# One more mix of half 1 on TensorE, and a new order of the work at the start on every engine

## The reference

```python
# layer 0: eight 256x256 weights mixed by cond, masked
w = einsum('bg,got->bot', cond, weight * mask)
x = x + (einsum('bnt,bot->bno', x, w) + bias)
# layer 1: a shared gated MLP and the best 2 of 8 experts by cond, inner size 1024
rw = softmax(cond); w, sel = top_k(rw, 2); w = w / w.sum()
x = x + mlp(x, shared) + sum_k w_k * mlp(x, expert[sel_k])
# mlp(x) = (gelu_tanh(x @ gate) * (x @ up)) @ down
```

## Time and profile before

| | us |
|---|---|
| median of 3 runs (lowest, highest) | 412.96 (412.57, 413.46) |
| profiled execution, its own time | 412.5 |
| its span | 410.7 |
| PE busy | 405.5 |
| POOL busy | 313.2 |
| DVE busy | 306.8 |
| ACT busy | 252.8 |

### The profile page before, as it was taken

One profiled execution on the slowest core, in us unless ns is written; L12 is line 12 of the kernel. 1 busy time (PEld: TensorE's weight loads), 2 busy tenths in 40 slices (PEclk: granted clock), 3 DMA queues, 4 the chain that ended last, 5 costly groups with the idle time before them and its releaser, 6 DMA issues.

```text
span 410.7 us, 7438 instructions
## 1 busy us (share of the span) xinstructions
PE 405.5 (99%) x2236; PEld 352.7 (86%) x2236; DVE 306.8 (75%) x516; ACT 252.8 (62%) x482; POOL 313.2 (76%) x322
## 2 busy tenths in 40 slices
PE   8999999999999999999999999999999999999997
PEld 5788888888888988888889888888888888888886
DVE  5778886586658887767677879857687677677784
ACT  5687677565565668555655666757455656676541
POOL 1699999999719689999635879999670977999630
PEclk9999999999999999999999999999999999999999
DMA  8543342333200622333000152222201042241101
GB/s 297 205 138 97 120 104 91 102 86 98 75 4 7 190 60 86 122 105 102 28 26 1 51 184 97 77 77 98 81 26 27 0 130 76 77 129 54 51 1 53
DMA packets 18895, 35.23 MB, mean 86 GB/s; under 512 B 2098, under 2 KB 2610, under 8 KB 18866
## 3 DMA queue, kind: packets, MB, share of 16 engines
q1 hardware_dynamic: 18576, 34.61, 26.7%
q10 hardware_dynamic: 290, 0.26, 0.2%
HBM read 32.77 MB, written 2.10 MB: 85 GB/s over the span
## 4 chain that ended last, share of the span: by engine, by line
PE 97%; DVE 2%; issue 0%; ACT 0%; POOL 0%; DVEq 0%; POOLq 0%
PE o_ps L582 16%; PE p_ps L582 12%; PE g_ps L528 11%; PE u_ps L527 11%; PE u_ps L531 10%; PE u_ps L528 10%; PE g_ps L527 10%; PE g_ps L531 10%; PE l_ps L481 2%; PE g_ps L653 1%; PE u_ps L430 1%; PE o_ps L622 0%; DVE t_raw L978 0%; DVE out_sb L1131 0%; DVE x_lo L1016 0%
## 5 line engine op out<-in xcount | busy, mean ns | idle before, releaser
L1237 POOL TENSOR_TENSOR eg_lo<-raw_g,eg_hi 128x512 fp32r<-128x512 f32 x64 | 92.5, 1468 | 11.1 <-ACT eg_hi L737 11.1
L766 ACT ACTIVATE gelu<-g_ps 128x512 f32<-128x512 f32 x95 | 56.9, 599 | 52.6 <-PE g_ps L531 50.9
L1054 DVE SCALAR_TENSOR_TENSOR u_ps<-gelu,route_cur,u_ps 128x512 f32<-128x512 f32 x64 | 48.1, 752 | 48.3 <-PE u_ps L531 45.0
L1090 DVE TENSOR_TENSOR h_lo<-t_raw,h_hi 128x1024 fp32r<-128x1024 f32 x46 | 81.3, 1766 | 0.5 <-ACT h_hi L799 0.5
L1279 POOL TENSOR_TENSOR ed_lo<-s_raw,ed_hi 128x512 fp32r<-128x512 f32 x30 | 54.6, 1821 | 0.0
L786 ACT CAST h_hi<-u_ps 128x256 fp32r<-128x256 f32 x46 | 17.2, 373 | 57.5 <-DVE t_raw L1069 42.4
L528 PE MATMUL g_ps<-x_hi,eg_lo 128*128 128x512 f32 (+1 forms) x128 | 50.2, 392 | 0.0
L527 PE MATMUL g_ps<-x_hi,eg_hi 128*128 128x512 f32 (+1 forms) x128 | 50.0, 391 | 0.0
L527 PE MATMUL u_ps<-x_hi,eg_hi 128*128 128x512 f32 (+1 forms) x128 | 49.8, 389 | 0.0
L528 PE MATMUL u_ps<-x_hi,eg_lo 128*128 128x512 f32 (+1 forms) x128 | 49.8, 389 | 0.0
L799 ACT CAST h_hi<-t_raw 128x1024 fp32r<-128x1024 f32 x46 | 47.9, 1040 | 0.4 <-DVE t_raw L1076 0.2
(11 more groups left out here) (230 smaller groups left out, 1147.8 us busy)
## 6 DMA issues: line engine op xcount, KB each, us to landing
raw_g<-experts SPq DMA_DIRECT2D x64, 256.0 KB, 2.7
raw_d<-experts SPq DMA_DIRECT2D x32, 256.0 KB, 2.7
raw_g<-shared SPq DMA_DIRECT2D x8, 256.0 KB, 5.7
l_raw<-l_w SPq DMA_DIRECT2D x3, 512.0 KB, 5.8
x_in<-xT SPq DMA_DIRECT2D x6, 256.0 KB, 3.2
outT<-out_sb SPq DMA_DIRECT2D x6, 256.0 KB, 3.0
raw_d<-shared SPq DMA_DIRECT2D x4, 256.0 KB, 3.2
x_in<-xT SPq DMA_DIRECT2D x1, 512.0 KB, 4.2
```

The source lines that it names most:

```text
L766: act.activation(gelu[:, s % 2], l0_ps if at_first(b) and s == 1 else g_ps, ACT.Gelu_apprx_tanh).then_inc(gelu_done, 1)
L1054: dve.scalar_tensor_tensor(u_ps[:, s % 2], gelu[:, s % 2], route_cur[:, k:k + 1], u_ps[:, s % 2], ALU.mult, ALU.mult).then_inc(h_done, 1)
L1090: dve.tensor_tensor(h_lo[:, at], t_raw[:], h_hi[:, at].bitcast(F32), ALU.subtract).then_inc(t_lo_done, 1)
L1237: pool.tensor_tensor(eg_lo[:, j % RING], raw_g[:, j % RAW_G], eg_hi[:, j % RING].bitcast(F32), ALU.subtract).then_inc(gu_lo_done, 1)
```

## The change

In words, by engine:

- PE: half 1's mixes are 2, 3, 5, 6, 7 (before: 2, 3, 5, 7) and stand together ahead of `first_layer_0`; both `pass_x_rest` stand ahead of them. `first_gate_up` uses x1_lo of a half right behind x1_hi of that half.
- DVE: `combine_0(1, 6)` is gone. `split_l0_0` stands behind the combines of half 1. `route_weigh` moves from ahead of `first_x1_lo` to between steps 0 and 1 of batch 0.
- ACT: `first_x1(0)` moves ahead of `split_b2(0, 0)`. In step 2 the casts of chunks 4 and 5 stand on either side of `first_x1(1)` and `split_t(0, 0)`, and `split_shared_s` stands behind `copy_b12` in steps 2, 4 and 6.
- POOL: the rest of chunk 4 is made ahead of the sums of pair 1's down weights, that of chunk 5 right behind them and ahead of pair 1's rests.

```diff
--- before.py
+++ after.py
@@ -257,9 +257,9 @@
         def chunks_at(s):
 
             if s == 1:
-                return range(4, 5)
+                return range(4, 6)
             if s == 3:
-                return range(5, 7)
+                return range(6, 7)
             if s == 5:
                 return range(7, 10)
             return range(s + 3, min(s + 5, CHUNKS + ECH))
@@ -451,8 +451,6 @@
                 pe.wait_ge(first_hi_done, 1)
                 for th in range(HH):
                     first_layer_part(l0_hi, 0, th, x_hi)
-                mix_l0(1, 5)
-                mix_l0(1, 7, last=True)
                 for th in range(HH):
                     first_layer_part(l0_hi, 0, th, x_lo)
                 pe.wait_ge(first_lo_done, 1)
@@ -513,13 +511,12 @@
                         at = off + hh * P
                         pe.wait_ge(lo_done, 1)
                         pe.matmul(ps, w_lo[:, at:at + P], x1_at(x1_hi, 0, hh), start=False, stop=False)
-                for ps, off, done in ((g_ps, GATE, g_done), (u_ps[:, 0], UP, u_done)):
-                    for hh in range(HH):
-                        if off == GATE:
-                            pe.wait_ge(x1_lo_done, hh + 1)
+                    pe.wait_ge(x1_lo_done, hh + 1)
+                    for ps, off, done in ((g_ps, GATE, g_done), (u_ps[:, 0], UP, u_done)):
                         at = off + hh * P
                         mm = pe.matmul(ps, w_hi[:, at:at + P], x1_at(x1_lo, 0, hh), start=False, stop=(hh == HH - 1))
-                    mm.then_inc(done, 1)
+                        if hh == HH - 1:
+                            mm.then_inc(done, 1)
 
             def project(ps, w_hi, w_lo, off, b):
                 for hh in range(HH):
@@ -668,10 +665,12 @@
             pass_x(1)
             mix_l0(0, 6)
             mix_l0(0, 7, last=True)
-            pass_x_rest(0)
+            for hh in range(HH):
+                pass_x_rest(hh)
             mix_l0(1, 2, first=True)
-            mix_l0(1, 3)
-            pass_x_rest(1)
+            for g in (3, 5, 6):
+                mix_l0(1, g)
+            mix_l0(1, 7, last=True)
             first_layer_0()
             first_gate_up()
             gate_up(0, 1)
@@ -820,7 +819,6 @@
                                 split_gu(0, c - CHUNKS)
                     if s % 2 == 0 and 0 < s < CHUNKS:
                         split_shared_d(s // 2)
-                        split_shared_s(s // 2)
                     if s >= CHUNKS and s % 2 == 0:
                         split_d(0, (s - CHUNKS) // 2)
                 else:
@@ -854,8 +852,8 @@
             def step(b, s, with_next):
                 activate(b, s)
                 if at_first(b) and s == 2:
-                    for oh in range(HH):
-                        first_x1(oh)
+                    split_shared(4)
+                    first_x1(1)
                 if s % 2 == 0 and s > 0 and fast(b, s // 2 - 1):
                     split_t(b, s // 2 - 1)
                 if not fast(b, s // 2):
@@ -863,9 +861,11 @@
                     split_h(b, s)
                 elif s % 2 == 0:
                     if at_first(b) and s == 2:
-                        weights_beside(b, 1)
+                        split_shared(5)
                     weights_beside(b, s)
                     copy_b12(b, s // 2)
+                    if at_first(b) and s < CHUNKS:
+                        split_shared_s(s // 2)
                 else:
                     split_b11(b, s // 2)
                     split_b2(b, s // 2)
@@ -919,6 +919,7 @@
             activate(0, 1)
             split_b11(0, 0)
             split_shared_s(0)
+            first_x1(0)
             split_b2(0, 0)
             batch(0, True)
             with act.Fori(1, B - 1) as b:
@@ -974,7 +975,7 @@
                 if first:
                     dve.tensor_scalar(acc, w, cond_all[:, 0, g:g + 1], None, ALU.mult).then_inc(first_mixed, 1)
                 else:
-                    dve.wait_ge(first_mixed, 4 * oh + {1: 1, 4: 2, 5: 3, 6: 3}[g])
+                    dve.wait_ge(first_mixed, 4 * oh + {1: 1, 4: 2, 5: 3}[g])
                     dve.scalar_tensor_tensor(acc, w, cond_all[:, 0, g:g + 1], acc, ALU.mult, ALU.add).then_inc(first_mixed, 1)
 
             def add_mixed_0():
@@ -989,7 +990,7 @@
 
             def add_mixed_1(th):
                 at = slice(D + th * P, D + (th + 1) * P)
-                dve.wait_ge(first_mixed, 8)
+                dve.wait_ge(first_mixed, 7)
                 dve.wait_ge(mixed, 2)
                 dve.tensor_tensor(l0_first[:, at], l0_first[:, at], mix_ps[1][:, th * P:(th + 1) * P], ALU.add).then_inc(first_added, 1)
 
@@ -1198,21 +1199,20 @@
             add_mixed_0()
             apply_mask_0()
             combine_0(1, 0, first=True)
-            split_l0_0()
             combine_0(1, 1)
             combine_0(1, 4)
-            combine_0(1, 6)
+            split_l0_0()
             for th in range(HH):
                 add_mixed_1(th)
                 apply_mask_1(th)
             for th in range(HH):
                 split_l0_1(th)
-            route_weigh()
             for oh in range(HH):
                 first_x1_lo(oh)
             route_index()
-            for s in range(2):
-                step(0, s, False)
+            step(0, 0, False)
+            route_weigh()
+            step(0, 1, False)
             batch(0, True)
             with dve.Fori(1, B - 1) as b:
                 batch(b, True)
@@ -1308,13 +1308,13 @@
                 for s in range(1, STEPS):
                     if s % 2:
                         p = (s + 1) // 2
-                        if s in (3, 5):
+                        if s in (1, 5):
                             split_shared(chunks_at(s)[0])
                         if p < PAIRS:
                             shared_s(p)
                         elif p < NP:
                             expert_s(0, p - PAIRS)
-                        for c in chunks_at(s)[1 if s in (3, 5) else 0:]:
+                        for c in chunks_at(s)[1 if s in (1, 5) else 0:]:
                             if c < CHUNKS:
                                 split_shared(c)
                             else:
```

## The result

The changed kernel is slower: 414.22 us in the median of 22 runs (413.26 to 416.61), the kernel before 412.84 in 22 runs. The ratio is 1.0034, with a 95% interval of 1.0025 to 1.0042, so 1.4 us more (1.0 to 1.7). The profiled execution took 414.03 us, its span is 412.2 us. All ratios in this document leave out four executions that took 817 to 2299 us, three of the kernel before and one of e5.

What follows compares the result with a forecast made beforehand. The prediction took the start plus a fixed stream of PE matmuls as the bound: -0.72 + 1.59 = +0.87 us, so the median goes from 412.96 to 413.8 us. The forecast's own range was 413.4 to 414.3, the whole range 412.2 to 415.1.

Steps and rivals of the forecast that it cites:

- What bounds the kernel: Whole kernel: its start plus a fixed stream of PE matmuls; a change moves the stream's start, removes waits or adds them.
- no other wait of PE: Sign to look for: PE has no new wait besides the one ahead of step 2's up projection.
- The hold of `route_weigh`: Between steps 0 and 1, running POOL instructions hold its DVE instructions; step 2's up projection waits 1.59 us more.
- T: The start of `first_x1_hi(1)`: 15.22 us before, forecast at 14.98; later times are counted from it.
- The second instruction's margin of 0.10 us: `route_weigh`'s second instruction is issued at T + 4.85, 0.10 us before chunk 3's rest starts, so it meets the last sum.
- the first rival: `route_weigh`'s second instruction misses the last sum and is held by chunk 3's rest: 1.26 us more, 415.1; chance 0.17.
- The second rival: `route_weigh`'s fourth instruction isn't held: 0.82 us less, 413.0, no change; chance 0.10.
- x1's rest sooner: Step 0: x1_lo comes sooner without `route_weigh` ahead of it, removing 0.48 us of PE's waits.
- The added mix: Start, half 1's mixes: weight 6 mixed on PE instead of DVE brings T 0.24 us sooner.
- The order of chunks 4 and 5: POOL and ACT, steps 2 to 5: keeps the gain by avoiding a 0.6 us wait; price zero, 0.3 at worst.
- The fourth rival: The new order costs elsewhere too (gelu of step 3, load of weights 6 and 7): 414.1; chance 0.05.
- The sum: Whole kernel: 0.72 us gained at the start, 1.59 more wait in step 2, +0.87 us in all.

Runs made afterwards that it cites:

- e5: e3 with the old order of chunks 4 and 5, of `first_x1` and of the casts of the sums; 413.30 us, ratio 1.0006.
- e7: e3 with POOL's `shared_s(1)` ahead of the rests of chunks 4 and 5; 412.51 us, ratio 1.0001.
- e8: e3 with ACT's `split_shared_s(1)` behind `activate(0, 3)` instead of at the end of step 2; 412.30 us, ratio 0.9985.
- e9: e3 with the edits of e7 and e8 together; 412.85 us, ratio 0.9991.
- e10: The same kernel as e8, measured again; 412.47 us, ratio 0.9988.
- e11: The same kernel as e7, measured again; 412.60 us, ratio 0.9983.
- e2: The changed kernel without the third instruction of `route_weigh`, the fourth adding `pair` in its place (experts' weights wrong by a factor); 413.20 us, ratio 1.0011.
- e3: The changed kernel with `route_weigh` moved earlier, right behind `split_l0_0`; 413.18 us, ratio 1.0004.
- e4: The changed kernel with weight 6 of half 1 mixed by DVE again and `split_l0_0` in its old place; 414.18 us, ratio 1.0027.
- e6: The changed kernel with `route_weigh` back ahead of `first_x1_lo`, as in the kernel before; 413.68 us, ratio 1.0022.
- e1: The changed kernel with POOL held back ahead of chunk 3's rest until `route_weigh` has ended; 413.57 us, ratio 1.0016.

## Why the prediction was right, and where it was off

- **What bounds the kernel, and the way the sum is made: right.** PE's stream from step 1 to the end has one length, 389.13 to 389.16 us in the kernel before, e7, e8, e9, e10 and e11. Every difference is the point where it starts and the waits in it. But "no other wait of PE" was among the signs, and there is one, at step 4.
- **The hold of `route_weigh`: right, in mechanism and size.** Forecast: the third instruction 1.21 and the fourth 0.94 us, 1.59 us more wait. Measured: 1.22 and 0.92, and 1.70 + 0.08 - 0.15 = 1.63. With T at 15.33, step 2's up projection starts at T + 8.30 (forecast T + 8.33). The Trainium skill ("SBUF — State Buffer", section "Who interferes with whom") says that a VectorE instruction with two SBUF inputs and a GpSimd instruction that reads SBUF shut each other out, and that the one issued second waits for the other's end; the runs agree for the scalar_tensor_tensor too, as e2 shows with 1.23 us, and POOL's sum of 1.46 us in e3 shows it the other way round.
- **The second instruction's margin of 0.10 us** was 0.15: issued 20.13, chunk 3's rest 20.28. It met the last sum as forecast; 0.15 us later it would have met chunk 3's rest, as in the first rival, so there is some luck in this. The second rival's price has a slip: the sum has the fourth instruction at 0.94 us, not 1.0, so not being held would have saved 0.77, not 0.82.
- **x1's rest sooner: right.** 0.48 forecast, B went down by 0.54. The 0.06 are PE's distances, 0.227 in the changed step 0 (12 from 15.13 to 17.85) instead of the 0.231 that I took from the old one.
- **The added mix: half the size, and not one number.** The term was 0.24, A went down by 0.11. The sum put the landing of weights 6 and 7 near 10.85 (it was 10.91 even in the kernel before) and the wait at 0.05. In the changed kernel's profile ten passes last 2.55 us; 0.38, nine distances of 0.215 and the late first follower make 2.40. I had allowed 0.05 of this 0.15. So the start now hangs on the landing, which DVE's queue hid before: in the kernel before and in e4 `add_mixed_1` starts 0.04 behind DVE's last combine (12.47 and 12.36), and A is 6.21 and 6.22. Where half 1's loads come early against half 0's mixes (e6) the new order gains 0.6 in A; where the load of weights 6 and 7 lands late (11.84 in e8, seventh pass at 11.97) it loses 0.05.
- **The order of chunks 4 and 5: wrong step.** I gave its price as "Zero, and 0.3 at worst" because the gelu of step 3 had 0.9 us to spare. It had none. Two things were left out: POOL waits 1.11 us for ACT's cast of chunk 4 (which stands behind the late gelu of step 2), and DVE's rest of 1024 columns holds one of the sums for 1.0 us. It costs 0.19 in the changed kernel and 0.68 with `route_weigh` out of the way, no less than the wait of 0.63 that it takes away (e5). The fourth rival named this place and the load of weights 6 and 7, without this cause, and got a chance of 0.05. Its 414.1 is nearer to the measured 414.22 than the forecast's 413.8: what happened is the forecast with this rival on top.
- **The sum.** 0.87 forecast; by the stretches 1.24; by the runs 1.40 (1.03 to 1.73). Of the 0.37 missing from the forecast, 0.19 is step 4, 0.13 the mix, -0.06 step 0, 0.04 the hold, and 0.07 of C stands at no single wait: against e7's stream, matmul by matmul, most of it is spread over the fifteen matmuls behind step 4's last late follower, and 0.03 lies near 42 us. So the direction and the largest term were understood, not guessed, but two smaller terms, 0.3 us together, were both taken too favourably.

## What to carry to other kernels

A gap on VectorE's own timeline isn't free room: each link of a chain of short VectorE instructions that read SBUF with two inputs, or as a tensor_scalar, can wait for another GpSimd instruction when GpSimd's queue is full (1.22 and 0.92 us for two links here), so put such a chain where GpSimd is idle (four times 0.17 us in e3 instead of 2.5 us in all). When an in-order queue is changed to bring one thing sooner, ask for each moved instruction which wait it takes with it and what stands behind that wait; ScalarE's cast of the sums took the gelu of the next step with it, although the cast itself wasn't urgent. And measure a change of several parts part by part: the start of this one gained 0.65 us, and two of its moves gave back 1.9, almost three times that.

## What the runs showed of the hardware

- A VectorE instruction held by GpSimd ends behind the recorded end of the GpSimd instruction by its own time less 0.14 us: by 0.02 to 0.03 us where it takes 0.17 alone, by 1.08 us where it takes 1.22 alone (the rest of 1024 columns; in e3 from 25.16 to 26.59, with a sum recorded until 25.51). So one issued in the last 0.14 us loses nothing: in the kernel before such a rest, issued at 25.55, took 1.23 us with a sum recorded until 25.68. That holds only if GpSimd pauses then: at 180.54, 0.06 us ahead of such an end and 0.01 ahead of GpSimd's next instruction, the same rest took 2.11 us.
- The first matmul of 512 columns behind a wait has its follower 0.31 to 0.34 us later instead of 0.23: each wait of PE costs 0.08 to 0.11 beyond itself.
- PE's passes of the mixes were 0.43 us apart up to about 8.0 us in the kernel before and 0.215 from then on. In e1 the slow distance held until 9.1 us, although the granted clock of those stretches reads 1.00 in both. Columns: length, busy time and count of PE, PEld, DVE, ACT, POOL, granted clock, DMA share, GB/s; then the passes of half 0's second group, which took 1.20 us in the kernel before.

```profile
7.00:8.00 1.00, 1.00 (x4) 0.62 (x3) 0.99 (x2) 1.00 (x1) 0.00 (x0) 1.00 0.94 371
8.00:9.00 1.00, 1.00 (x3) 0.81 (x3) 0.52 (x2) 0.24 (x2) 0.00 (x0) 1.00 1.05 348
```

```profile
7.77 1.92 PE L430 MATMUL u_ps<-l_raw,out_sb 128*128 128x256 f32 x4
```

  That 1.00 is no reading: the first clock record of each trace, full speed, stands at 7.91 us in the kernel before, 8.10 in the changed one, 9.54 in e1 and 12.62 in e9, where the distance halves, and ahead of it there is none. Twice the distance fits the lower of the two levels, 1.2 instead of 2.4 GHz, but no record here shows that level at the start. So "full throughout", said of the kernel before, is shown from 7.91 us on.

  In e1 this cost some 0.13 us: the ten passes end 2.82 us behind the landing of half 1's first load (9.49) instead of 2.69 in the changed kernel (9.78). In e9's profile it held on, the ten passes took 3.15 us instead of 2.55, and its A is 6.56. What decides when the clock rises no run here shows.
